# A graph kernel's first phase in fp32: one transpose a tile, halved products, two tiles of seven on ScalarE

## The reference

```python
h  = relu(layernorm(x))                                    # 100000 x 32
xs = concat(h[src, :8], h[dst, :8])                        # E x 16 scalars
xv = concat(h[src, 8:].reshape(E, 8, 3), h[dst, 8:]...)    # E x 16 vectors of 3
w  = (relu(emb @ W1) @ W2).reshape(E, 7, 16, 8)            # weights of each edge, by way of 16 hidden units
s_out = xs.wa_s + (xv.y1).wb_s      g_out = xs.wa_g + (xv.y1).wb_g
v_out = (xs, y1).wc + xv.wd + (xv, y2).we
x = x + segment_sum([tanh(s_out), tanh(g_out) * v_out] * norm, dst)
```

## Time and profile before

| | |
|---|---|
| runs | 1195.46 us median of 3 (1193.73 to 1196.26) |
| profiled execution, its own time | known by its span: 1442.6 us from first to last instruction |
| phase one, middle, phase two in the profile | about 55 to 762, 762 to 1092, 1092 to 1442.6 us |
| TensorE clock granted, mean | 0.76 |
| busy share of the span | DVE 68%, PE 59%, ACT 58%, POOL 55%, PEld 48% |

### The profile page before, as it was taken

The page is one execution under the profiler, slowest core; times in us unless marked ns, Lnnn a source line. Parts: engine busy times, 40 slices in busy tenths (PEclk is TensorE's granted clock), DMA queues, the critical chain, the costliest instruction groups (busy, mean ns, idle before and its releaser), DMA issues.

```text
span 1442.6 us, 16871 instructions
## 1 busy us (share of the span) xinstructions
PE 856.9 (59%) x5248; PEld 690.5 (48%) x5248; DVE 982.3 (68%) x1799; ACT 842.4 (58%) x2035; POOL 794.9 (55%) x796
## 2 busy tenths in 40 slices
PE   0256777677776877777874221323135777777773
PEld 0245665566565756666773110211123565555552
DVE  4566686777776667566664635865336999998984
ACT  0346665666766575666754333746244887787871
POOL 5664565466554665455004455775752665656664
PEclk9988688878777777767786555555557999999986
DMA  4121021111111102111014213432300000000000
GB/s 114 19 56 35 16 50 22 43 28 46 58 41 29 37 10 62 34 36 23 16 52 163 76 37 84 115 109 76 88 20 5 10 9 9 9 9 9 9 9 7
DMA packets 40669, 60.52 MB, mean 42 GB/s; under 512 B 17361, under 2 KB 31077, under 8 KB 40324
## 3 DMA queue, kind: packets, MB, share of 16 engines
q1 hardware_dynamic: 12216, 46.86, 10.2%
q0 software_dynamic: 25184, 12.32, 5.4%
q10 hardware_dynamic: 3180, 0.26, 0.2%
HBM read 40.33 MB, written 19.37 MB: 41 GB/s over the span
## 4 chain that ended last, share of the span: by engine, by line
PE 21%; ACT 21%; DVE 20%; another core or an unknown queue 16%; DVEq 10%; issue 8%; SPq 1%; DMA 1%; POOL 0%; POOLq 0%
PE sums L1080 9%; ACT h1d_or_products L809 5%; DVEq L1764 4%; PE tens L1070 3%; ACT below L900 3%; PE turnB L1056 3%; PE turnA L1056 2%; ACT stack_turned L800 2%; DVEq L1705 2%; DVE run L1753 2%; ACT agg_or_stacks L800 2%; DVE tens L1725 2%; PE tens L1074 2%; DVE dcen L1748 1%
## 5 line engine op out<-in xcount | busy, mean ns | idle before, releaser
L674 POOL DMA_INDIRECT x_rows<-in_x,src_index x196 | 196.1, 1001 | 228.9 <-PE tens L1074 146.3
L701 POOL DMA_INDIRECT out_dram<-agg_or_stacks,scatter_index x196 | 193.6, 988 | 144.6 <-ACT agg_or_stacks L974 90.4
L694 POOL DMA_INDIRECT agg_or_stacks<-run_sums,sum_row_index x196 | 203.1, 1036 | 112.3 <-issue 57.9
L674 POOL DMA_INDIRECT x_rows<-in_x,dst_index x196 | 197.2, 1006 | 64.9 <-issue 64.9
L1408 DVE TENSOR_TENSOR h1d_or_products<-tens,hid 128x768 f32<-128x768 f32 x168 | 158.8, 952 | 64.8 <-PE tens L1074 42.8
L1080 PE MATMUL sums<-h1d_or_products,ident 128*128 128x192 f32 x896 | 174.4, 356 | 4.8 <-issue 4.2
L1080 PEld LDWEIGHTS sums<-h1d_or_products,ident 128*128 128x128 f32 x896 | 164.9, 212 | 11.3 <-issue 11.1
L1143 PE MATMUL sums<-one_column,halves_or_steps 128*128 128x1 f16 x112 | 22.1, 197 | 176.6 <-DVE halves_or_steps L1564 62.0
L967 ACT ACTIVATE features_or_rows<-stack_turned,is_last 128x132 f32<-128x132 f32 x196 | 85.9, 520 | 39.3 <-DVE stack_turned L1735 39.3
L1143 PEld LDWEIGHTS sums<-one_column,halves_or_steps 128*128 128x128 f16 x112 | 14.1, 126 | 197.7 <-ACT below L900 73.2
L1070 PE MATMUL tens<-w_scalar_stacks,agg_or_stacks 96*128 96x384 bf16 x196 | 66.5, 432 | 65.9 <-ACT h1d_or_products L809 41.4
(11 more groups left out here) (308 smaller groups left out, 2536.5 us busy)
## 6 DMA issues: line engine op xcount, KB each, us to landing
src_everywhere<-src_by_columns SPq DMA_DIRECT2D x14, 896.0 KB
xin<-in_x SPq DMA_DIRECT2D x27, 449.5 KB
out_dram<-xin SPq DMA_DIRECT2D x27, 449.5 KB
x_rows<-in_x,src_index POOLq DMA_INDIRECT x196
x_rows<-in_x,dst_index POOLq DMA_INDIRECT x196
run<-run_sums SPq DMA_DIRECT2D x1, 3136.0 KB
agg_or_stacks<-run_sums,sum_row_index POOLq DMA_INDIRECT x196
out_dram<-agg_or_stacks,scatter_index POOLq DMA_INDIRECT x196
```

Source lines behind the costliest of these rows:

```text
L674: nc.gpsimd.indirect_dma_start(xs[:, t, side, :], None, x, bass.IndirectOffsetOnAxis(ap=idx[:, t:t + 1], axis=0)).then_inc(s_gath[g % LEAD ...
L694: nc.gpsimd.indirect_dma_start(aggr[:, t, :], None, rs, bass.IndirectOffsetOnAxis(ap=ridx[:, t:t + 1], axis=0)).then_inc(s_rsg[t // GA], 16)
L701: nc.gpsimd.indirect_dma_start(out, bass.IndirectOffsetOnAxis(ap=sidx[:, t:t + 1], axis=0), aggr[:, t, :], None, bounds_check=N - 1, oob_i ...
```

## The change

Phase one works in fp32 throughout. There is no splitting into parts, neither of the rows nor of W2. The five units of a tile (80 numbers) are transposed together, in fp32, one transpose a tile, in two lots of four and three tiles, and each lot is copied by ACT once. A tile's product is two fp32 matmuls of 384 columns, with W2 padded by zeros to 80 rows. ACT multiplies tiles 2 and 5, DVE the five others. DVE halves all seven tiles, in two instructions (tiles 0 to 2, then 3 to 6, the second after tile 6), and TensorE sums a group with 8 fp32 matmuls of 336 columns (16 records), in the following group, after product 2. The transposes of the next group move to before product 5 and before product 6. SP has 3 transfers of W2 in place of 18; DVE sets the two weight tiles to zero at the start; POOL's pace for tiles 14 to 19 waits for other events.

```diff
-    TACT = 3
-    CH = 7
-    NCH = UNITS * GA // CH
+    BY_ACT = (2, 5)
+    FIRST = 3
+    TURNS = ((0, 4), (4, GA))
...
-            def first_parts(n):
-                act.wait_ge(s_h, n + 1)
-                nc.scalar.copy(stack[:, :, 0:SLOTS:2, :], spread(hflat, 2, [P, UNITS * GA, 3, VU])).then_inc(s_hi, 1)
-            def second_parts(n):
-                act.wait_ge(s_r1, n + 1)
-                nc.scalar.copy(stack[:, :, 1:4:2, :], spread(rest, 2, [P, UNITS * GA, 2, VU])).then_inc(s_mid, 1)
...
+            def turned(n, b, half):
+                of = slice(TURNS[half][0] * P, TURNS[half][1] * P)
+                act.wait_ge(s_turn, n * 2 + (half + 1))
+                nc.scalar.copy(stackT[b][:, of], turn[half][0:KU, 0:of.stop - of.start]).then_inc(s_turned, 1)
+            def multiply(g, b, t):
+                act.wait_ge(s_tens, g * GA + (t + 1))
+                if past(g, 0):
+                    act.wait_ge(s_half, g * 2 - 1 + (t >= FIRST))
...
+                multiply(g, b, BY_ACT[0])
                 if next2:
                     square(g + 2)
                 if g in SLICE1:
                     dense_square(SLICE1[g])
+                if past(g, 0):
+                    gates(g - 1)
                 if next1:
                     hidden(g + 1, 1 - b)
-                    turned(g + 1, 1 - b, range(2))
+                multiply(g, b, BY_ACT[1])
+                if next1:
+                    turned(g + 1, 1 - b, 0)
...
+            def turn_units(n, half):
+                pe.wait_ge(s_h, n + 1)
...
+                for t in range(first, end):
+                    mm = nc.tensor.transpose(turn[half][0:KU, (t - first) * P:(t - first + 1) * P],
+                                             hrow[:, t].rearrange("p u c -> p (u c)"), ident[:])
...
+                rows = stackT[b][:, t * P:(t + 1) * P]
+                nc.tensor.matmul(bank[:, 0:HID * OG], rows, w_s[:]..., start=True, stop=True)
+                nc.tensor.matmul(bank[:, 512:512 + HID * OG], rows, w_v[:]..., start=True,
+                                 stop=True).then_inc(s_tens, 1)
+            def sum_units(g):
+                pe.wait_ge(s_half, g * 2 + 2)
...
+                for j in range(HID // 2):
+                    mm = nc.tensor.matmul(sums[:, 0:GA * OUTS].rearrange("p (c o) -> p c o", o=OG), ident[:],
+                                          half[:, :, j, :], start=(j == 0), stop=(j == HID // 2 - 1))
...
-                turn_units(g, b, range(2, 4))
-                if past(g, 0):
-                    sum_first(g - 1)
-                turn_units(g, b, range(4, NCH))
                 product(g, b, 2)
                 if past(g, 0):
-                    sum_rest(g - 1)
+                    sum_units(g - 1)
                 product(g, b, 3)
...
                 product(g, b, 4)
+                if more:
+                    turn_units(g + 1, 0)
                 product(g, b, 5)
                 if more:
-                    turn_units(g + 1, 1 - b, range(2))
+                    turn_units(g + 1, 1)
                 product(g, b, 6)
...
-                multiply(g, b, 2)
+                multiply(g, b, 3)
                 if past(g, 0):
                     outputs(g - 1, 1 - b)
-                halve(g)
-                if next1:
-                    third_part(g + 1)
+                halve(g, True)
+                multiply(g, b, 4)
                 if past(g, 0):
                     messages(g - 1, 1 - b)
-                multiply(g, b, 4)
-                multiply(g, b, 5)
...
                 multiply(g, b, 6)
+                halve(g, False)
```

More of the change, by code:

```diff
@@ L321, in build_gnn @@
         at = 0
-        w2s = part(h1d_area, at, HID, OG, parts=SC)
-        at += HID * OG
         w2d = part(h1d_area, at, HID, MOUT, parts=VU)
@@ L597, in _ @@
             sp.wait_ge(s_w2p, 1)
-            for place, which in enumerate((0, 0, 1, 1, 2, 0)):
-                rows = slice(place * VU, (place + 1) * VU)
-                for u in range(2):
-                    sp.dma_start(w_s[rows, u, :, :], w2s_part[u * VU:(u + 1) * VU, which]).then_inc(s_w2, 16)
-                sp.dma_start(w_v[rows, :, :], w2v_part[:, which]).then_inc(s_w2, 16)
+            for k in range(3):
+                sp.dma_start(w_v[(k + 1) * VU:(k + 2) * VU, :, k * MOUT:(k + 1) * MOUT], w2v).then_inc(s_w2, 16)
             for g, d in SLICE1.items():
@@ L729, in _ @@
             load(w2e, w2_rows[WE])
[L730 removed]
+            for rows, plan in ((slice(0, VU), (WA_S, WA_G, WC)), (slice(KU - VU, KU), (WB_S, WB_G, WE))):
                 for col, which in enumerate(plan):
[L732 removed]
+                    load(w_s[rows, :, col * MOUT:(col + 1) * MOUT], w2_rows[which])
             for t in range(GA):
@@ L830, in _ @@
             deviation(0)
-            first_parts(0)
-            second_parts(0)
             take_emb(0)
@@ L1033, in _ @@
             pe.wait_ge(s_feat, 16 * 9)
+            pe.wait_ge(s_w2p, 1)
             pe.wait_ge(s_w2, 16 * N_STACKS)
@@ L1128, in _ @@
             group(NP - 1, 1)
-            sum_first(NG - 1)
-            sum_rest(NG - 1)
+            sum_units(NG - 1)
             def search(c, pairs):
@@ L1387, in normalize, with halve @@
                 v.tensor_reduce(hrow[:, :, 4, :], vprod, AX, ALU.add).then_inc(s_h, 1)
-            def first_rest(n):
-                dve.wait_ge(s_hi, n + 1)
-                v.tensor_tensor(rest, hflat, stack[:, :, 0, :], ALU.subtract).then_inc(s_r1, 1)
-            def third_part(n):
-                dve.wait_ge(s_mid, n + 1)
-                v.tensor_tensor(stack[:, :, SLOTS - 1, :], rest, stack[:, :, 1, :], ALU.subtract).then_inc(s_lo, 1)
-            def halve(g):
-                v.drain()
-                if past(g, 0):
-                    dve.wait_ge(s_sumA, g)
-                v.tensor_tensor(first_half, prod[:, 0:2 * TACT, 0:HID // 2, :],
-                                prod[:, 0:2 * TACT, HID // 2:, :], ALU.add).then_inc(s_half, 1)
+            def halve(g, first):
+                v.drain()
+                if first:
+                    if past(g, 0):
+                        dve.wait_ge(s_sum, g)
+                    at = slice(0, 2 * FIRST)
+                    n = sum(t < FIRST for t in BY_ACT)
+                else:
+                    at = slice(2 * FIRST, NR)
+                    n = NACT
+                if past(g, 0) or past(n, 0):
+                    dve.wait_ge(s_tact, g * NACT + n)
+                v.tensor_tensor(half[:, at], prod[:, at, 0:HID // 2, :], prod[:, at, HID // 2:, :], ALU.add
+                                ).then_inc(s_half, 1)
             def multiply(g, b, t):
@@ L1465, in _ @@
             normalize(0)
-            first_rest(0)
-            third_part(0)
             dense_sums(0)
```

190 lines of the change are left out of this document (59 added, 131 removed).

## The result

The changed kernel takes 1210.24 us (median of 4, 1209.03 to 1213.01) against 1195.62 for the kernel before: a ratio of 1.0135, interval 1.0113 to 1.0157. It is slower by 1.35%, where 1150 us had been forecast.

What follows compares the result with a forecast made beforehand. The prediction took the order of waits between engines, not any engine's total, as the bound. Phase one's groups -36, start -7 and end -2 made -45, from 1195.5 to 1150 us, range 1118 to 1205.

Steps and rivals of the forecast that it cites:

- 28 x (19.3 - 20.6) = -36: Phase one: 28 groups falling from a mean of 20.6 to 19.3 us, 36 us saved.
- The 0.2 us for stretches at half clock: Phase one: allowance a group for TensorE at half clock, raising the new group from 19.1 to 19.3 us.
- The chain as walked: New group's sequence through the engines: 18.3, 18.5 or 20.8 us by slice steps, 19.1 on average.
- the clock, slower: Rival: fp32 products in phase one run at lower clock, 1248 or 1352 us; even at clock 0.84. Chance 0.13.
- The 14.1 us in one piece: TensorE's unbroken busy stretch in each new group, likened to phase two, where the clock was 0.98.
- The base of 20.6 us: Old group's pace in timed runs: mean of 21 groups at 20.34 us and 7 at 21.4.
- The check (55 + 574 + 220 + 350 = 1199): Whole old kernel: start, 28 groups, middle less unexplained waits, and phase two, near the median of 1195 us.
- Engines' sums: Busy time a new group: ACT 13.1 us, DVE 17.1, TensorE 15.9 at full clock.
- The second tile on ScalarE: Tile 5 on ACT, 3.17 us; its rival: ACT reaches it 1.5 us late, 1172 us, no change. Chance 0.17.
- Start: Before the first groups: no splitting and fewer W2 copies save 7 us, bounds 11 and 1.
- End: Last sums of phase one: 8.5 us become halving 1.8 and sum 4.7, 2.0 us saved.
- The unexplained waits: Phase one while POOL gathers: 231 us of waits on an unknown queue, taken as the profiled execution's alone.

Runs made afterwards that it cites:

- e2: Changed kernel plus six idle fp32 matmuls a group in TensorE's pauses, two before product 6 and four after: 1166.13 us, 0.9765 of the kernel before.
- e1: The kernel before, unchanged, run again for a second profile: 1190.88 us, profiled span 1185.2 us.
- e4: The kernel before plus nine idle fp32 matmuls a group on TensorE ahead of product 5: 1165.23 us, 0.9772 of the kernel before.
- e3: Changed kernel with tile 5 multiplied by VectorE again, ScalarE keeping tile 2 alone: 1236.82 us, ratio 1.0354.
- e9: Changed kernel unmodified, on a chip where the kernel before takes 1414.64 us: 1329.54 us, 0.9488 of the kernel before.
- e16: Changed kernel with only the four idle matmuls behind product 6, on a chip where before takes 1426.47 us: 1333.35 us, ratio 0.934.
- e7: Changed kernel with six idle matmuls a group right ahead of the sum, bridging no pause; before took 1422.47 us on that chip: ratio 0.9766.
- e17: Changed kernel with seven of 14 gathers a group left out, on a chip where before takes 1191.55 us: 1205.84 us, ratio 1.012.
- e15: The kernel of e2 repeated on a chip where the kernel before takes 1426.47 us: 1334.65 us, ratio 0.935.
- e18: Changed kernel with product operands in one bf16 each and seven of 14 gathers a group left out: 1141.68 us, ratio 0.9586.

## Why the prediction was wrong

**The step that failed** is 28 x (19.3 - 20.6) = -36. It came out as 28 x (20.46 - 19.67) = +22, on both sides of the minus sign.

*The 0.2 us for stretches at half clock.* The chain as walked was good: 18.3, 18.5 and 20.8 us, mean 19.1; at a held clock e2 shows 17.6, 18.6 and 20.0, mean 18.95 with three half-clock stretches left in. But a stretch comes in nearly every group, and they cost 1.5 us a group, not 0.2. This is 1.2 us a group, 33 us. It is the rival "the clock, slower", given 0.13, and its numbers were right: a mean clock of 0.84, at which it put the chain at 20.9; 20.46 was measured. What spoke against it, a longest pause of 2.2 us, did not count: 1.13 us at most was enough here. The 14.1 us in one piece that were to hold the clock hold nothing, since the fall comes inside them and doubles each product. The section "HAM oscillation — how this bites in real kernels" of the Trainium skill's page "TensorE: Matmul & The Clock Gate" tells of a kernel in which waits for DMA of some 3 to 5 us bring half clock back in every round. That it comes back in every round the trace bears out, with a stretch in 23 of 24 groups; but the pauses here are far shorter, 1.13 us at most in the boundary shown.

*The base of 20.6 us.* It was read from one group free of unexplained waits. That group, at a clock of 0.83, was one with a half-clock stretch in it. In e1 the groups spread from 17.8 to 21.2 us by where the stretch falls, mean 19.67: 0.9 us a group, 26 us. The check (55 + 574 + 220 + 350 = 1199) could not show it. What lies behind phase one was taken right, 570 us, and is 569.7 in e1 (from its last read of the sums at 615.5 us to the end); up to there it had 629. Groups 0 and 1 of e1, 26.4 and 22.6 us long, hid part of the shorter pace, and the 14 us by which the check exceeds e1's span of 1185 were only 4 against the median.

**Engines' sums were right.** ScalarE 317.1/24 = 13.2 us a group (13.1 forecast), VectorE 400.6/24 = 16.7 (17.1), 0.5 less than before (0.6 forecast), sum 4.5 at full clock (4.7), product 1.29 (1.36), the larger halving 1.76 (1.81). TensorE at full clock would be some 15.5 (412.6/24 in e2 less 1.7 of fill; 15.9 forecast). But ScalarE's 3 us were not on what sets the pace once the clock is held: before takes the same 18.95 us with them. What does set it differs by group. With all slice steps VectorE is busy 19.0 of 20.0 us in e2 (19.6 and 1.2 of drains had been forecast); without slice steps only 13.6 of 17.4 (group 25, `534.60:552.00`), and there the chain through all engines decides, which the change made only 0.2 us shorter (17.35 us against 17.57 in e4):

```profile
534.60:552.00 17.40, 16.56 (x67) 10.60 (x66) 13.55 (x24) 12.49 (x46) 1.89 (x2) 1.00 0.11 29
```
```profile
534.80:552.40 17.60, 15.78 (x139) 14.19 (x139) 14.09 (x27) 15.34 (x35) 0.00 (x0) 1.00 0.08 24
```

POOL's 14 gathers, one behind the other, take the same 17.6 us in e2 (18.6 had been estimated), so on a held clock a shorter chain would have gained little more.

**The second tile on ScalarE** did not cost what its rival feared (e3 is slower without it), but the copy that stands behind it is what TensorE waits for in the pause of 1.13 us. **Start:** the first multiplication comes at 46.2 us against 48.9, -2.7 instead of -7, and it is lost again by group 2 (+1.6). **End:** -2.0 was forecast, +2.4 came with all that lies behind group 26. **The unexplained waits** were taken for the profiled execution's. They come with the chip, or with the call in which it was used, for each chip served one: three showed them in timed runs (1414 to 1426 us), two did not. That the gain there would be larger the forecast did say (span of some 1350; e9 has 1333).

Open: what the waits behind "remote" are, whether they hang on POOL's gathers, and why the changed kernel has so few of them in phase one; whether the pause ahead of product 0 alone lets the clock fall; what the halved sum alone does on the first kind of chip, where it was not run.

## What to carry to other kernels

Before trading many short matmuls for fewer fp32 ones, price TensorE's time of each at half clock, where they stand on the chain, and look in the granted clock for how often the stretch comes. Read a pace from many groups, never from one, and compare it at one and the same clock. If pauses of a microsecond bring half clock back in every round, matmuls without use in those pauses can be worth more than a rebuilt group, as they were on the first kind of chip; try them first, on more than one chip.

## What was not expected of the hardware

- Pauses of 0.70 and 1.13 us in a TensorE that is busy 91% of the time are followed by 6.8 us at half clock. With the second one filled to 0.22 (e16, groups 24 to 26) none follows. Stretches of 10.2 us come in e3 with three pauses, but also in e7.
- The stretches of the changed kernel begin 20.5 us apart from group 2 to group 19 (385.4, 405.9, 426.4), although its groups are 19.5 to 21.5 us long by turns. On a chip with waits (e9) and with half the gathers gone (e17) groups 3 to 19 have the same lengths within 0.1 us.
- The same kernel takes 1191 to 1196 us on some chips and 1414 to 1426 us on others, and a change can lose 1.3% on the first and gain 5% on the second. In phase one the extra waits are seen only while POOL gathers: in e15 a group without gathers takes 17.4 us, one with them up to 24.6.
- A product of two bf16 matmuls takes 0.33 us at full clock (e18), the same in fp32 1.29, a factor of 3.9. The Trainium skill, "FP8 and Floating Point Precision", section "TensorE Precision Notes", has fp32 as four passes; the runs agree.
